# Result rows named ahead of the pieces, and the first result chunk combined ahead of the last shared chunk

## What is computed

```python
x = x + 0.5 * _L2_ffn_ref(_layernorm(x), ...)   # 8 routed experts, top 2, and a shared expert z
x = x + 0.5 * _L3_ffn_ref(_layernorm(x), L3_ffn_weight, L3_ffn_bias)  # 6-bit block rounding, then one product
x = x + _L3_attn_ref(_layernorm(x), L3_attn_Wqkv, L3_attn_Wout)       # softmax in blocks of 32
x = x + 0.5 * _L3_ffn_ref(_layernorm(x), L3_ffn_weight, L3_ffn_bias)
```

## Time and profile before

| what | value |
|---|---|
| time, median of 3 runs | 2970.96 us (2967.53 to 2971.29) |
| profiled execution, span | 3096.7 us |
| mean granted TensorE clock, share of full | 0.901 |
| busy, share of the span | PE 83%, DVE 67%, ACT 57%, POOL 38% |
| last piece stored, by the timeline | 2752.4 us |
| last shared chunk added, by the timeline | 2770.1 us |
| first PE work of mix3, by the timeline | 2796.3 us |

### The profile page before, as it was taken

One profiled execution on the slowest core, in us unless ns is written; L12 is line 12 of the kernel. 1 busy time (PEld: TensorE's weight loads), 2 busy tenths in 40 slices (PEclk: granted clock), 3 DMA queues, 4 the chain that ended last, 5 costly groups with the idle time before them and its releaser, 6 DMA issues.

```text
span 3096.7 us, 67889 instructions
## 1 busy us (share of the span) xinstructions
PE 2568.8 (83%) x25429; PEld 2019.4 (65%) x25429; DVE 2087.5 (67%) x7733; ACT 1780.5 (57%) x3496; POOL 1188.1 (38%) x1634
## 2 busy tenths in 40 slices
PE   7899988659599668467679999999999996975786
PEld 4467764446377446345469999999889884643555
DVE  6667757753377743573378888888888885435677
ACT  5344446323255333244469999999999983543453
POOL 4200003555523546565552332322343335445312
PEclk9799989879799779778889999999999997996897
DMA  9900000013210024224300000000001001420001
GB/s 238 287 4 3 3 3 1 20 54 118 79 42 8 31 71 124 75 71 145 123 24 14 19 20 13 20 13 13 21 30 34 20 20 51 137 96 28 19 3 29
DMA packets 149543, 164.59 MB, mean 53 GB/s; under 512 B 15713, under 2 KB 123874, under 8 KB 149218
## 3 DMA queue, kind: packets, MB, share of 16 engines
q1 hardware_dynamic: 120770, 85.53, 10.1%
q0 software_dynamic: 28448, 74.71, 7.6%
HBM read 85.18 MB, written 75.01 MB: 52 GB/s over the span
## 4 chain that ended last, share of the span: by engine, by line
PE 38%; DVE 10%; issue 4%; another core or an unknown queue 3%; POOL 2%; ACT 2%; DMA 0%; DVEq 0%; ACTq 0%; POOLq 0%
PE banks L3564 6%; PE banks L3549 6%; PE banks L3494 3%; PE banks L3511 2%; PE banks L3530 2%; PE banks L3503 2%; PE banks L3487 1%; PE banks L3529 1%; PE banks L3247 1%; PE banks L3258 1%; PE banks L3260 1%; PE banks L3249 1%; PE banks L3248 1%; PE banks L3520 1%
## 5 line engine op out<-in xcount | busy, mean ns | idle before, releaser
L3564 PE MATMUL banks<-layer,shared_floats 128*128 128x128 f32 x2048 | 292.0, 275 | 0.0
L3665 POOL TENSOR_SCALAR shared_floats<-shared_floats 128x2 f32<-128x2 f32 x256 | 57.7, 225 | 583.6 <-DVE shared_floats L3656 580.2
L3564 PEld LDWEIGHTS banks<-layer,shared_floats 128*128 128x128 f32 x2048 | 258.8, 192 | 0.0
L3549 PE MATMUL banks<-shared_floats,layer 128*128 128x256 f32 x1024 | 243.9, 381 | 0.0
L3954 ACT ACTIVATE shared_floats<-banks,layer 128x256 f32<-128x256 f32 x512 | 210.3, 471 | 50.9 <-PE banks L3549 49.4
L1394 POOL DMA_INDIRECT results<-shared_floats,e_token_rows x160 | 155.2, 970 | 125.5 <-ACT shared_floats L1375 81.6
L3549 PEld LDWEIGHTS banks<-shared_floats,layer 128*128 128x128 f32 x1024 | 185.9, 192 | 20.2
L3667 POOL TENSOR_TENSOR shared_floats<-shared_floats,neg_half 128x2 f32<-128x2 f32 x256 | 183.7, 717 | 21.3
L3677 DVE TENSOR_SCALAR shared_floats<-banks,shared_floats 128x128 f32<-128x128 f32 x512 | 185.5, 404 | 7.3 <-POOL shared_floats L3667 7.3
L2163 DVE TENSOR_REDUCE shared_floats<-banks 128x2 f32<-128x512 f32 (+3 forms) x256 | 110.6, 484 | 94.5 <-PE banks L2027 93.0
L255 PE MATMUL banks<-ident,xn 128*128 128x128 f32 x320 | 61.8, 325 | 126.3 <-issue 76.5
(11 more groups left out here) (444 smaller groups left out, 8044.9 us busy)
## 6 DMA issues: line engine op xcount, KB each, us to landing
bins<-zero SPq DMA_DIRECT2D x1, 18176.0 KB, 70.0
layer<-in_dram_layers SPq DMA_DIRECT2D x16, 902.0 KB
bins<-layer SPq DMA_DIRECT2D x16, 650.0 KB, 12.6
shared_floats<-bins SPq DMA_DIRECT2D x32, 325.0 KB
expert_weights<-in_dram_experts SPq DMA_DIRECT2D x32, 312.0 KB
results<-results SPq DMA_DIRECT2D x32, 256.0 KB
results<-zero SPq DMA_DIRECT2D x1, 4096.0 KB, 16.1
bins<-xn,f_bin_row POOLq DMA_INDIRECT x256
```

Source lines behind the costliest of these rows:

```text
L3549: m = T.matmul(k.bank[5 + half][:, part], w["w1"][:, tile(n)], h1[:, :], start=True, stop=True)
L3564: m = T.matmul(to, hidden[:, n * S + t * P:n * S + (t + 1) * P], w["w2"][:, tile(n)], start=False, stop=(n == NF - 1), skip_group_check=True)
```

## The change

Three things. First, the names of result chunks 0 and 1 are written by DVE ahead of the pieces of ffn2 instead of at the start of mix3. Second, `gather_in` becomes a function of the module, and the one for chunk 0 moves from mix3's start into `pieces_vector`, between `shared8_finish` of chunk 6 and that of chunk 7. Third, `combine_first` waits for its own chunk of x to be done instead of all eight. POOL's, ACT's and PE's functions are not changed.

```diff
     def precede(self, later):
         self.next = later if later.early else None
+        self.rounded_next = later.rounding if later.kind == "mix3" else None
@@ combine_first
     if part[0] == 0:
-        V.wait_ge(k.sem("x_done"), s.x0)
+        V.wait_ge(k.sem("x_done"), s.x0 - NC + i + 1)
         wait_results(k, V, n)
@@ mix3_vector
-    name_result_rows(k, f, 0)
-    name_result_rows(k, f, 1)
-    gather_in(0)
     quantise_weight(k)
     quantise_scaled(0)
-    gather_in(1)
+    gather_in(k, f, 1)
     finish(0, k.bank[6])
@@
+def gather_in(k, s, i):
+
+    name_and_combine(k, s, i)
+    ln_stats(k, s, i, s.results0 + i + 1)
@@ pieces_vector
+    rounded = s.rounded_next
+    if rounded:
+        for i in range(RESULT_RING):
+            name_result_rows(k, rounded, i)
     for m in range(m0, m0 + PIECES):
         multiply(m)
...
         shared8_multiply(k, s, i)
         if i > behind[0]:
             shared8_finish(k, s, i - 1)
+    if rounded:
+        gather_in(k, rounded, 0)
     for i in behind[-1:]:
         shared8_finish(k, s, i)
```

More of the change, by code:

```diff
@@ L133, in __init__ @@
         self.results0, self.before, self.after_routed = max(done - 1, 0) * NC, before, before in ("ffn1", "ffn2")
-        self.next, self.early, self.places = None, EARLY.get((before, kind), 0), range(NC)
+        self.next, self.rounded_next, self.early, self.places = None, None, EARLY.get((before, kind), 0), range(NC)
         self.sent_early = len(IN_SECOND_PASS) if (before, kind) == ("att2", "ffn2") else 0
@@ L2569, in add_out @@
         V.tensor_tensor(x, k.bank[2][:, S:2 * S], x, ALU.add).then_inc(k.sem("x_done" if n % 2 else "at_added"), 1)
-    def gather_in(i):
-        name_and_combine(k, f, i)
-        ln_stats(k, f, i, f.results0 + i + 1)
     def quantise_scaled(i, between=None):
@@ L2600, in mix3_vector @@
     finish(1, k.bank[7])
-    gather_in(2)
+    gather_in(k, f, 2)
     for n in range(B + 1):
@@ L2613, in mix3_vector @@
         if on and not odd and at + 1 < NC:
-            gather_in(at + 1)
+            gather_in(k, f, at + 1)
         if on and not odd and at >= NC:
```

## The result

The changed kernel takes 2955.96 us (median; 2944.06 to 2961.06), the kernel before, run beside it, 2969.32 us (2961.19 to 2973.54). The ratio is 0.9949, with a 95% interval of 0.9938 to 0.9961: 13.4 us faster, where 15.5 were forecast, and 2955.96 us where 2955.5 were. The total is met more closely than the gain, because before's median came out 1.6 us lower beside it.

A forecast was written before the change was run, and what follows sets the result against it. At the seam, POOL's row of gathers, held back by names late in DVE's program, was taken as the bound. Names 0, gathers' start -15.7, meeting DVE's sums +0.2, rest 0: -15.5, from 2970.96 to 2955.5 us; range 2949 to 2963.

The forecast's parts named there:

- The names ahead of the pieces: Two DVE casts before the first piece cost 0, hidden by 4.19 us idle; POOL's gathers start 15.7 us earlier.
- The landing of the last store: Before POOL's first gather: the store lands 2.0 us after its issue ends, so POOL starts at 2755.4 (2754.9 to 2755.6).
- bound (a): Thirteen gathers issued beside DVE work, two meeting the combine: 0.25 to 0.9 us slower, taken at 0.2.
- Enough time for the gathers: At DVE's first combine: chunk 0's gathers ready at 2766.65, DVE there at 2767.86, so 1.2 us to spare.
- the meeting of POOL and DVE: At POOL's first norm step: POOL free at 2771.55, DVE's sums at 2771.6; the step starts at 2771.7, 15.5 us earlier.
- What is late next: Behind POOL's first norm step all engines do the same work at the same distances, so all is 15.5 us earlier.
- the rest 0: In the sum, everything besides the gathers' start (-15.7) and the meeting with DVE's sums (+0.2) adds 0 us.
- bound (b): PE's clock behind the seam: two matmul groups take 3.78 or 1.98 us each, 3.6 us either way; taken as 0.
- Part 2: First combine ahead of the last addition: its wait met with 1.2 us to spare, combine to norm sums from 2767.9 to 2771.6.
- The starving of PE: Rival in mix3: PE stalls about 11 us beside gathers; one stall gives 2966.5, two 2977.5 (two: chance 0.04).
- the gathers don't start early: Rival: POOL's start hangs on another semaphore in fetch_results, so the 15.7 us stay, 2971; chance 0.04.
- A late landing: Rival: last store or gathers 3 us later, DVE waits before its last addition; 12.5 us gained, 2958.5; chance 0.06.

The follow-up runs named there:

- e1: The kernel before plus only the names moved ahead of the pieces, first combine staying at mix3's start, looser x_done wait included; 2956.2 us, ratio 0.9958 against before.
- e4: The changed kernel with five idle POOL instructions between the fourth and fifth gather of chunk 0; 2961.19 us, ratio 0.9969 against before.
- e0: The kernel before, unchanged, profiled again; 2967.52 us, ratio 1.000, span 2964.4 us.
- e3: The changed kernel, unchanged, profiled again; 2954.97 us, ratio 0.9954 against before.
- e2: The kernel before plus only the first combine moved ahead of the last addition, names directly in front of it, looser x_done wait included; 2963.01 us, ratio 0.9983.
- e6: The changed kernel with POOL's norm step of attention chunk 0 put ahead of the last three gathers of chunk 2; 2950.61 us, ratio 0.9928 against before.
- e9: The changed kernel with 21 and 13 extra unread matmuls ahead of PE's two longest waits; 2959.33 us, ratio 0.9961 against before.
- e11: The changed kernel with 12 and 11 extra unread matmuls ahead of PE's two longest waits; 2952.54 us, ratio 0.9937 against before.
- e10: The changed kernel with POOL's attention norm step ahead of three gathers, plus 12 and 6 extra unread matmuls on PE; 2947.46 us, ratio 0.9920 against before.

## Why the prediction held, step by step

**Which wait bounds the seam: right.** POOL's idle time before the gathers was the thing to remove. e1, which removes it alone, has nearly the whole gain, and e4, which puts some of it back, loses as much as it puts back.

**The names ahead of the pieces: right, they cost nothing.** The way from the start of the addition in front of the pieces to the start of DVE's first multiply in them takes 4.88 us in before and e0, without the names there, and 4.88 in e1, with them. In after and e3 it takes 8.49, but in e2, which has no names there, 8.37. First after's timeline, then e1's, then e2's:

```profile
2538.30 0.63 PE L3238 MATMUL banks<-ident,shared_floats 128*128 128x128 f32 x4 [3.01 <-DMA shared_floats<-bins,piece_rows]
2543.92 1.54 DVE L3294 SCALAR_TENSOR_TENSOR shared_floats<-banks,expert_weights,shared_floats 128x512 f32<-128x512 f32 x2 [7.65 <-ACT shared_floats L3339]
```

```profile
2544.77 1.54 DVE L3295 SCALAR_TENSOR_TENSOR shared_floats<-banks,expert_weights,shared_floats 128x512 f32<-128x512 f32 x2 [4.00 <-ACT shared_floats L3338]
```

```profile
2548.74 1.54 DVE L3294 SCALAR_TENSOR_TENSOR shared_floats<-banks,expert_weights,shared_floats 128x512 f32<-128x512 f32 x2 [7.68 <-ACT shared_floats L3338]
```

In after, e3 and e2 PE waits some 3 us for the rows of the first piece, which POOL gathers. These 3.6 us lie ahead of the last store, outside the ledger. They are no cost of the names; why they stand in these three traces and not in the others is open.

**The landing of the last store: the mis-sized term.** I took 2.0 us from the end of its issue, from scatters of an earlier group. POOL's idle time before the first gather is 3.57 us in after, 3.61 in e3, 3.04 in e1, 3.17 in e4, 3.21 in e6, 3.05 in e9 and 2.55 in e11: all longer than my upper end of 2.2. POOL's start moved by 14.16 us instead of 15.7. A nearer row was in before's trace and I had not looked for it: the same pair, a store of result rows and a gather of results behind it, stands at the end of the first run of ffn2. Under the view of the store's line (L3383 in before, L3389 in after), "who waited for it (us, times)", before and then after have:

```profile
  POOL results L1474: 2.6, 1
```

```profile
  POOL results L1475: 6.2, 2
```

2.6 us in the first run; the changed kernel adds its own 3.6. Taking 2.6 in place of 2.0 would have given 15.1 us for the start of the gathers.

**The gathers beside DVE: right.** Those that overlap the combine took 0.95 and 1.06 us in after's timeline, so bound (a) stayed under 0.2 us. By the Trainium skill (SBUF — State Buffer, Summary: rules for kernel authors) the second of the two to issue would have been blocked until the first had finished. The gathers' rows don't bear that out: the one of 0.95 us ends within L1511's 1.15. POOL's small norm instructions do: L197 takes 0.24 us by itself (2689.78 in after), and 0.82 where DVE's L885, with two inputs in SBUF, runs from 2696.05 to 2696.74; it ends at 2696.16 + 0.82 = 2696.98, behind L885. So the rule was cited against the wrong instructions of POOL.

**Enough time for the gathers, and the meeting of POOL and DVE: right, with one shift that I had not foreseen.** No wait stands at the combine. But the addition of chunk 6 ends 1.7 us later in after, e3 and e2, and 3.3 in e10, because PE's granted clock fell while it did that chunk. Where it did not fall (e6, e9), the combine comes at 15.51 and 15.37 us, against 15.45 foreseen, and the norm step at 20.16 and 20.01, against 19.3: here POOL is the later of the two, because of the landing (its gathers start at 4.17 and 4.01 us, against 3.0). Where it fell, DVE is the later, at 20.85 in after, but only just: POOL waited 0.21 us for DVE's sums there, so it was ready itself at 20.64. So of the 1.7 us that the seam gave less than forecast (13.84 against 15.5) some 1.3 are the landing and 0.2 the clock in chunk 6; the rest is that e0's norm step stands 0.15 us nearer to its store than in the rows.

**What is late next, and "the rest 0": right for the change, and bound (b) is shown.** The ledger is a pure shift behind the norm step. That it is one owes something to luck: the two groups of L2388 that I had named (3.78 or 1.98 us) ran at the low clock in both traces of before and in both of after, and not in all of the experiments. The way from ACT's norm of attention chunk 0 to the addition of rounded chunk 1 takes 15.08 us in after (3.78 and 3.66), 13.40 in e1 (3.78 and 1.98) and 11.15 in e11 (1.98 twice). That is 3.93 us between the ends, for an estimate of 3.6; 3.5 of it are the two groups, the rest the turn ahead of them (L256, 1.12 us in after and 0.66 in e11).

**Part 2 was over-explained.** I gave it a step of its own, and it is worth 1.2 to 2.0 us in the traces and nothing that the timed runs can show. Without it the norm step waits for DVE (e1: 2.04 us), with it DVE and POOL meet: it only pays as much as POOL's own row of gathers lets it.

**The rivals.** The starving of PE fell with e0. That the gathers don't start early fell with after's timeline. A late landing came about half as far as priced (1.6 of 3 us), and in another place: DVE's combine still waits for nothing, but where the clock doesn't fall POOL is now the later at the norm step. In the range, the 3.4 us of spread reach only from the median to the lowest of the three runs; from lowest to highest it is 3.8.

**What stays open.** Why the landing takes 2.55 us in one trace and 3.6 in another, and why PE's clock falls in chunk 6 in after, e3, e2 and e10 and not in the others, most of which have the same instructions up to there. Three of these four, all but e10, are also those in which PE waits for the rows of the first piece. Neither was settled by a run.

## What to carry to other kernels

If an engine waits for a few cheap instructions that stand late in another engine's program only by habit, move those first: two casts of DVE gave nearly all of this gain, and the larger move beside them gave one to two microseconds. When one wait goes, price the one behind it from the same pair of instructions elsewhere in the trace, not from a similar pair, and then look at the order of the engine that is late next; here a swap of POOL's order showed 2.5 us more in the trace. Profile the kernel before twice ahead of explaining a stall of 11 us: one execution may hold stalls that the kernel does not have.

## What the runs showed of the hardware

**PE's clock fell in chunk 6 in some executions.** Windows of after, then of e1, at the same distance from the last store; columns as in the earlier trace rows:

```profile
2658.00:2662.00 4.00, 2.05 (x12) 1.22 (x11) 1.50 (x2) 2.52 (x4) 2.17 (x3) 1.00 0.07 16
2662.00:2666.00 4.00, 4.00 (x12) 2.33 (x11) 0.69 (x1) 0.00 (x0) 3.08 (x4) 0.57 0.23 55
```

```profile
2658.90:2662.90 4.00, 2.05 (x13) 1.27 (x12) 1.49 (x2) 2.52 (x4) 2.75 (x3) 1.00 0.14 33
2662.90:2666.90 4.00, 3.36 (x13) 1.55 (x12) 1.37 (x2) 1.29 (x2) 2.97 (x4) 1.00 0.20 49
```

PE had been busy for 2.05 of the 4 us before in both; then it was granted 0.57 of 2.4 GHz, near its level of 1.2 GHz, in the one and all of it in the other. The gathers are not the cause: e1 has them then without the fall, and e2, where POOL is idle then, shows the same fall:

```profile
2662.80:2666.80 4.00, 2.05 (x12) 1.21 (x12) 1.49 (x2) 2.52 (x4) 0.00 (x0) 1.00 0.00 0
2666.80:2670.80 4.00, 4.00 (x12) 2.34 (x11) 0.69 (x1) 0.00 (x0) 0.00 (x0) 0.57 0.00 0
```

**What standing costs PE afterwards, and what useless work gives back.** In after PE stands 10.49 us at L850 and 8.99 at L256, and the two groups of L2388 behind these then cost 3.78 + 3.66 us. With 12 and 11 extra matmuls in those gaps they cost 1.98 each, 3.5 us less. The same trick with too many matmuls gave nothing (e9: last addition of rounded chunk 7 at 199.58 us, against 198.88 in after).

**The end of the kernel varies by the clock as well.** One of PE's matmul rows for the last chunk and DVE's last wait for PE, in after and then in e6:

```profile
2949.82 0.39 PE L863 MATMUL banks<-weightT,shared_floats 128*128 128x128 f32 x2
2951.14 0.69 DVE L939 SCALAR_TENSOR_TENSOR x<-banks,x 128x512 f32<-128x512 f32 x1 [2.67 <-PE banks L863]
```

```profile
2948.17 0.63 PE L863 MATMUL banks<-weightT,shared_floats 128*128 128x128 f32 x2
2950.54 0.69 DVE L939 SCALAR_TENSOR_TENSOR x<-banks,x 128x512 f32<-128x512 f32 x1 [5.36 <-PE banks L863]
```

The wait is 2.69 us longer in e6, but not the time, as DVE came to it sooner: from the last addition of rounded chunk 7 to this one takes 97.57 us in after and 98.90 in e6, 1.33 more, at a place that the changes don't touch. Such phases are one part of what executions differ by, and a reason to read the 1 to 2 us of part 2 from traces and not from times. They are not the largest: of the 3.1 us between the profiled executions of after and e3, 2.96 lie ahead of the last store (2654.69 and 2657.65).
